# A mixture-of-experts stage padded to 256 slots per step: pairs of tiles share one first-layer matmul and one gelu

## What is computed

```python
gate_logits = x_flat @ gate_w.T
topk_vals, topk_idx = jax.lax.top_k(gate_logits, K)          # K = 2 of E = 8
topk_w = jax.nn.softmax(topk_vals, axis=-1)
...
for e in range(E):
    h = jax.nn.gelu(x_flat @ w1[e].T + b1[e], approximate=False)   # 128 -> 512
    y = h @ w2[e].T + b2[e]                                        # 512 -> 128
    out = out + comb[:, e:e + 1] * y
```

## Time and profile before

| | us |
|---|---|
| median of 3 timed executions | 423.61 |
| lowest and highest of these | 418.68, 425.56 |
| the profiled execution, its own time | 420.72 |
| its span (first to last instruction) | 418.8 |

### The profile page before, as it was taken

The page is one execution under the profiler, slowest core; times in us unless marked ns, Lnnn a source line. Parts: engine busy times, 40 slices in busy tenths (PEclk is TensorE's granted clock), DMA queues, the critical chain, the costliest instruction groups (busy, mean ns, idle before and its releaser), DMA issues.

```text
span 418.8 us, 5584 instructions
## 1 busy us (share of the span) xinstructions
PE 306.1 (73%) x1879; PEld 216.8 (52%) x1879; DVE 215.9 (52%) x457; ACT 159.8 (38%) x497; POOL 233.0 (56%) x214
## 2 busy tenths in 40 slices
PE   4988999799797309988759587586595883976244
PEld 1335443434236205467659487485584883975222
DVE  3733999999468897224324353143242441532066
ACT  4433020210125875035335363253453552634162
POOL 9100677979104340176767777767777777576300
PEclk9999897979998855599988999999999899899755
DMA  8900000000000150011111111111111111121296
GB/s 333 419 2 0 2 0 0 2 0 0 1 2 0 51 144 8 1 50 39 44 43 45 46 38 48 46 37 51 40 40 42 46 45 47 34 42 42 75 291 239
DMA packets 19484, 25.47 MB, mean 61 GB/s; under 512 B 2941, under 2 KB 15230, under 8 KB 19200
## 3 DMA queue, kind: packets, MB, share of 16 engines
q1 hardware_dynamic: 14336, 12.40, 9.4%
q0 software_dynamic: 4544, 8.86, 7.6%
q10 hardware_dynamic: 576, 3.86, 2.2%
HBM read 16.72 MB, written 8.85 MB: 61 GB/s over the span
## 4 chain that ended last, share of the span: by engine, by line
PE 45%; ACT 14%; DVE 13%; issue 9%; another core or an unknown queue 6%; DMA 6%; POOL 4%; SPq 2%; DVEq 0%; POOLq 0%
PE PS L1092 13%; PE PS L1099 12%; ACT MV L558 8%; DVE PR L689 4%; PE PS L1077 4%; PE PS L987 3%; ACT SCR L524 3%; PE PS L939 3%; PE PS L973 2%; DMA PR<-token_rows,dsti 2%; DMA X<-x 2%; POOL expert_rows L419 2%; SPq L345 2%; PE PS L1034 2%
## 5 line engine op out<-in xcount | busy, mean ns | idle before, releaser
L558 ACT ACTIVATE MV<-PS,SCR 128x128 f32<-128x128 f32 x284 | 81.3, 372 | 115.3 <-PE PS L1092 72.3
L1099 PE MATMUL PS<-SCR,MV 128*128 128x128 f32 x568 | 82.9, 291 | 48.3 <-ACT MV L558 33.6
L1099 PEld LDWEIGHTS PS<-SCR,MV 128*128 128x128 f32 x568 | 72.9, 201 | 57.0 <-ACT MV L558 40.3
L419 POOL DMA_INDIRECT expert_rows<-PR,dsti x71 | 80.6, 1135 | 37.7 <-issue 19.3
L413 POOL DMA_INDIRECT PR<-token_rows,dsti x71 | 76.5, 1077 | 40.9 <-issue 40.6
L1092 PE MATMUL PS<-MV,SCR 128*128 128x128 f32 x568 | 78.7, 284 | 0.0
L859 DVE TENSOR_TENSOR PR<-PS,SCR 128x128 f32<-128x128 f32 x71 | 20.6, 290 | 105.7 <-remote 61.6
L366 POOL TENSOR_TENSOR PR<-PR 128x1024 f32<-128x1024 f32 x21 | 49.5, 2362 | 42.9 <-DVE PR L689 41.2
L867 DVE COPY SCR<-WALL 128x1156 f32 x71 | 55.7, 788 | 34.1 <-DVE PR L859 23.2
L1092 PEld LDWEIGHTS PS<-MV,SCR 128*128 128x128 f32 x568 | 73.0, 201 | 0.0
L689 DVE TENSOR_TENSOR PR<-RX,PS 128x512 f32<-128x512 f32 x66 | 41.8, 677 | 5.1 <-PE PS L973 5.0
(11 more groups left out here) (167 smaller groups left out, 316.0 us busy)
## 6 DMA issues: line engine op xcount, KB each, us to landing
SCR<-expert_rows SPq DMA_DIRECT2D x16, 256.0 KB, 5.3
WALL<-experts SPq DMA_DIRECT2D x1, 2312.0 KB, 19.6
WALL<-experts ACTq DMA_DIRECT2D x1, 2312.0 KB, 19.8
token_rows<-SCR SPq DMA_DIRECT2D x4, 512.0 KB, 3.2
out<-PR SPq DMA_DIRECT2D x8, 256.0 KB, 2.4
PR<-token_rows,dsti POOLq DMA_INDIRECT x71
expert_rows<-PR,dsti POOLq DMA_INDIRECT x71
X<-x ACTq DMA_DIRECT2D x2, 512.0 KB, 6.2
```

The costliest lines, as they stand in the source:

```text
L419: nc.gpsimd.indirect_dma_start(yr, bass.IndirectOffsetOnAxis(ap=dsti[:, 2, q:q + 1].bitcast(U32), axis=0), YS[:, q % NR, :], None, bounds_ ...
L558: last = nc.scalar.activation(GF[:, q % 2, c * P:(c + 1) * P], PS[:, 2 + q % 2, c * P:(c + 1) * P], ACT.Gelu, bias=part(q, "b1")[:, c:c + 1])
L1099: last = nc.tensor.matmul(PS[:, 4 + q % 4, 0:C], GF[:, q % 2, c * P:(c + 1) * P], part(q, "w2")[:, c * C:(c + 1) * C], start=(c == 0), sto ...
```

## The change

The slots of an expert are now padded to a multiple of 256, so that two neighbouring tiles always belong to the same expert. They form a pair j, and all work but the transposes, the gathers and the scatters is done per pair. There are `NJ = (2 * T + E * 255) // 256 = 39` pairs, so 78 tiles for the 71 before.

- TensorE: `hidden(j)` is four matmuls that stream 256 columns each, into two PSUM banks; `output(j)` is eight matmuls (two tiles by four chunks) and newly waits for the add of pair j - 2, as results now share two banks and not four. `turn(j)` is two transposes.
- ScalarE: four gelus of 256 columns and one copy of 256 per pair.
- DVE: one weight copy per pair, and one add of 256 columns. The tile counts per expert are computed with 255 and a shift by 8, then doubled.
- GpSimd: 78 gathers and 78 scatters. Only the even ones wait, and they wait for their pair. `SLAG` is 8.
- The list of TensorE is `hidden(j)`, `turn(j + 2)`, `output(j - 1)` as before, with j a pair.

```diff
-NQ = (2 * T + E * (P - 1)) // P
+PAIR = 2 * P
+NJ = (2 * T + E * (PAIR - 1)) // PAIR
+NQ = 2 * NJ
...
-        XT = MV[:, 1, 0:4 * P].rearrange("p (s n) -> p s n", s=4)
-        GF = MV[:, 0, :].rearrange("p (s n) -> p s n", s=2)
+        XT = MV[:, 1, :].rearrange("p (s n) -> p s n", s=4)
+        GF = MV[:, 2:4, :]
...
-        SLAG = 7
+        SLAG = 8
...
+        def hidden_out(j, c):
+
+            at = (c % 2) * PAIR
+            return PS[:, 2 + 2 * (j % 2) + c // 2, at:at + PAIR]
...
             def gather(q):
-                if q >= NR:
-                    pool.wait_ge(xt_done, q - NR + 1)
+                if q >= NR and q % 2 == 0:
+                    pool.wait_ge(xt_done, (q - NR) // 2 + 1)
                     pool.sem_inc(pool_held, 1)
...
             def scatter(q):
-                pool.wait_ge(ys_done, q + 1)
-                pool.sem_inc(pool_held, 1)
+                if q % 2 == 0:
+                    pool.wait_ge(ys_done, q // 2 + 1)
+                    pool.sem_inc(pool_held, 1)
...
-            def gelu(q):
-                act.wait_ge(h_done, q + 1)
+            def gelu(j):
+                act.wait_ge(h_done, j + 1)
                 for c in range(HC):
-                    last = nc.scalar.activation(GF[:, q % 2, c * P:(c + 1) * P], PS[:, 2 + q % 2, c * P:(c + 1) * P],
-                                                ACT.Gelu, bias=part(q, "b1")[:, c:c + 1])
+                    last = nc.scalar.activation(GF[:, j % 2, c * PAIR:(c + 1) * PAIR], hidden_out(j, c),
+                                                ACT.Gelu, bias=part(j, "b1")[:, c:c + 1])
...
-            def finish(q):
-
-                dve.wait_ge(y_done, q + 1)
-                if q >= NR:
-                    dve.wait_ge(y_out[q % NR], 16 * (q // NR))
-                nc.vector.tensor_tensor(YS[:, q % NR, :], PS[:, 4 + q % 4, 0:C], part(q, "b2"), ALU.add).then_inc(ys_done, 1)
+            def finish(j):
+
+                dve.wait_ge(y_done, j + 1)
+                s = 2 * j % NR
+                if 2 * j >= NR:
+                    for r in (s, s + 1):
+                        dve.wait_ge(y_out[r], 16 * (2 * j // NR))
+                nc.vector.tensor_tensor(YS[:, s:s + 2, :], PS[:, 6 + j % 2, 0:2 * C].rearrange("p (i n) -> p i n", i=2),
+                                        part(j, "b2").unsqueeze(1).to_broadcast([P, 2, C]), ALU.add).then_inc(ys_done, 1)
...
-            def turn(q):
-
-                pe.wait_ge(g_in[q % NR], 16 * (q // NR + 1))
-                last = nc.tensor.transpose(PS[:, q % 2, 0:P], GX[:, q % NR, :], prm_("ident"))
+            def turn(j):
+
+                for i in range(2):
+                    q = 2 * j + i
+                    pe.wait_ge(g_in[q % NR], 16 * (q // NR + 1))
+                    last = nc.tensor.transpose(PS[:, j % 2, i * P:(i + 1) * P], GX[:, q % NR, :], prm_("ident"))
                 last.then_inc(xt_done, 1)
...
-            def output(q):
-                pe.wait_ge(gelu_done, q + 1)
-                for c in range(HC):
-                    last = nc.tensor.matmul(PS[:, 4 + q % 4, 0:C], GF[:, q % 2, c * P:(c + 1) * P],
-                                            part(q, "w2")[:, c * C:(c + 1) * C], start=(c == 0), stop=(c == HC - 1))
+            def output(j):
+                pe.wait_ge(gelu_done, j + 1)
+                if j >= 2:
+                    pe.wait_ge(ys_done, j - 1)
+                for i in range(2):
+                    for c in range(HC):
+                        a = c * PAIR + i * P
+                        last = nc.tensor.matmul(PS[:, 6 + j % 2, i * C:(i + 1) * C], GF[:, j % 2, a:a + P],
+                                                part(j, "w2")[:, c * C:(c + 1) * C], start=(c == 0), stop=(c == HC - 1))
                 last.then_inc(y_done, 1)
```

More of the change, by code:

```diff
@@ L319, in build, with part @@
         WLEAD = 2
-        SLAG = 7
-        def part(q, name):
+        SLAG = 8
+        def part(j, name):
             a, b = WX[name]
-            return WE[:, q % 4, a:b]
+            return WE[:, j % 4, a:b]
+        def hidden_out(j, c):
+            at = (c % 2) * PAIR
+            return PS[:, 2 + 2 * (j % 2) + c // 2, at:at + PAIR]
         block = ctx.enter_context(nc.Block())
@@ L548, in _, with turned @@
             nc.scalar.preload_act_table_set("gelu_and_others")
-            def turned(q):
-                act.wait_ge(xt_done, q + 1)
-                nc.scalar.activation(XT[:, q % 4, :], PS[:, q % 2, 0:P], ACT.Copy).then_inc(xtc_done, 1)
-            def gelu(q):
-                act.wait_ge(h_done, q + 1)
+            def turned(j):
+                act.wait_ge(xt_done, j + 1)
+                nc.scalar.activation(XT[:, j % 4, :], PS[:, j % 2, 0:PAIR], ACT.Copy).then_inc(xtc_done, 1)
+            def gelu(j):
+                act.wait_ge(h_done, j + 1)
                 for c in range(HC):
-                    last = nc.scalar.activation(GF[:, q % 2, c * P:(c + 1) * P], PS[:, 2 + q % 2, c * P:(c + 1) * P],
-                                                ACT.Gelu, bias=part(q, "b1")[:, c:c + 1])
+                    last = nc.scalar.activation(GF[:, j % 2, c * PAIR:(c + 1) * PAIR], hidden_out(j, c),
+                                                ACT.Gelu, bias=part(j, "b1")[:, c:c + 1])
                 last.then_inc(gelu_done, 1)
[L562 to L567, removed]
+            for j in range(TLEAD):
+                turned(j)
+            for j in range(NJ):
+                gelu(j)
+                if j + TLEAD < NJ:
+                    turned(j + TLEAD)
             act.wait_ge(gates_done, 2)
-            act.wait_ge(y_done, NQ)
+            act.wait_ge(y_done, NJ)
             for b in range(B):
@@ L805, in _ @@
             ntl, tend, off = (e8[:, k, :] for k in range(3))
-            chain(nc.vector.scalar_tensor_tensor(e8i[:, 0, :], ends, float(P - 1), begin, ALU.add, ALU.subtract))
-            chain(nc.vector.tensor_scalar(e8i[:, 1, :], e8i[:, 0, :], 7, None, ALU.arith_shift_right))
-            chain(nc.vector.tensor_copy(ntl, e8i[:, 1, :]))
+            chain(nc.vector.scalar_tensor_tensor(e8i[:, 0, :], ends, float(PAIR - 1), begin, ALU.add, ALU.subtract))
+            chain(nc.vector.tensor_scalar(e8i[:, 1, :], e8i[:, 0, :], 8, None, ALU.arith_shift_right))
+            chain(nc.vector.tensor_scalar(ntl, e8i[:, 1, :], 2.0, None, ALU.mult))
             chain(nc.vector.tensor_tensor_scan(tend, ntl, ntl, 0.0, ALU.add, ALU.max))
@@ L873, in _ @@
                 dve.wait_ge(rows_out[b], 16)
[L874 to L880, removed]
+            for j in range(WLEAD):
+                take_expert(j)
+            for j in range(NJ + OLAG):
+                if j + WLEAD < NJ:
+                    take_expert(j + WLEAD)
+                if j >= OLAG:
+                    finish(j - OLAG)
             dve.wait_ge(gates_done, 2)
@@ L1091, in hidden @@
                 for c in range(HC):
-                    last = nc.tensor.matmul(PS[:, 2 + q % 2, c * P:(c + 1) * P], part(q, "w1")[:, c * P:(c + 1) * P],
-                                            XT[:, q % 4, :], start=True, stop=True)
+                    last = nc.tensor.matmul(hidden_out(j, c), part(j, "w1")[:, c * P:(c + 1) * P],
+                                            XT[:, j % 4, :], start=True, stop=True)
                 last.then_inc(h_done, 1)
-            def output(q):
-                pe.wait_ge(gelu_done, q + 1)
-                for c in range(HC):
-                    last = nc.tensor.matmul(PS[:, 4 + q % 4, 0:C], GF[:, q % 2, c * P:(c + 1) * P],
-                                            part(q, "w2")[:, c * C:(c + 1) * C], start=(c == 0), stop=(c == HC - 1))
-                last.then_inc(y_done, 1)
@@ L1103, in _ @@
[L1103 to L1111, removed]
+            def output(j):
[7 more added lines that the diff above has]
+                                                part(j, "w2")[:, c * C:(c + 1) * C], start=(c == 0), stop=(c == HC - 1))
+                last.then_inc(y_done, 1)
@@ L1113, in _ @@
+            for j in range(TLEAD):
+                turn(j)
+            for j in range(NJ + OLAG):
+                if j < NJ:
+                    hidden(j)
+                if j + TLEAD < NJ:
+                    turn(j + TLEAD)
+                if j >= OLAG:
+                    output(j - OLAG)
             for b in range(B):
```

16 lines of the change are left out of this document (8 added, 8 removed).

## The result

The changed kernel takes 558.48 us (median of four runs, 556.57 to 559.20) against 423.25 us for the kernel before in the same comparison: a ratio of 1.324, with a 95% interval of 1.318 to 1.330. The forecast was 550 us. The profiled execution took 556.57 us for a span of 554.7.

The account below looks back on a forecast made before the run. A closed loop through GpSimd's and TensorE's lists was to bind the changed kernel: start 190.9, 35 rounds of 9.05 us (316.8), end 13.1, rest 27.05 and 1.9, giving 550 us against 420.72; range 506 to 591.

Parts of the forecast that it names:

- second layer 0 starts: Front of the stage: the first second layer waits for gather 7 and wider sorting, so starts at 190.9 us.
- 35 rounds: Expert stage, second layer 0 to 35: one closed loop per pair, 9.05 us each, 316.8 us.
- from there to the end of the span: After the last scatter starts: nothing changes, 27.05 us more to the span's end.
- The order decides: GpSimd and TensorE lists: second gather queues behind a scatter awaiting an add, closing a loop walked once per pair.
- The links of the round: Loop from second layer through add, scatter, gather, landing and transpose to the next second layer: 8.05 us.
- The clock: TensorE's second layer behind each pause meets the low 1.2 GHz level: 1.0 us more a round, making 9.05.
- The rival in which the clock holds: TensorE stays at full clock, the round stays 8.05 us: 515 us in all, chance 0.25.
- The end: Second layer 35, first layer 38, three second layers and last scatters: 13.1 us, last scatter starting at 520.8.
- Gelu and DMAs: Work per engine: four gelus 1.6 us a pair, 14 more GpSimd DMA instructions 18 us; none decides.
- The late results: Rival: each round's add comes 3 us late, the round is 12.05 us, 655 us in all; chance 0.06.
- the ring: Expert stage: the closed loop of second layer, add, scatter, gather, landing and transpose, walked once per pair, 8.05 us unthrottled.
- Issue-bound: Rival: the loop closes within GpSimd's 5.2 us a round, its 156 DMA instructions bind, 410 us; chance 0.04.

Follow-up runs that it names:

- four experiments: Changed kernel with both gathers first, scatters ten tiles behind, or second layer before transposes: 446.21, 451.11, 453.59 us; kernel before with scatters 3 tiles behind: 733.88 us.
- Filling the pause: Changed kernel with 24 unused matmuls of 256 fp16 columns before each pair's transposes: 523.58 us.
- the ring opened: Changed kernel with both gathers before both scatters, scatters ten tiles behind, or TensorE's second layer before the transposes: 446.21, 451.11 and 453.59 us.
- the exchange of two neighbours: Changed kernel with both gathers of a pair issued ahead of both scatters on GpSimd: 446.21 us.
- fp16 kernel: Kernel before with the operands of both expert layers in fp16, biases and sums in fp32: 416.33 us, ratio 0.986.
- filled pair kernel: Changed kernel with 24 unused matmuls of 256 fp16 columns in TensorE's pause before each pair's transposes: 523.58 us.
- Rings: Kernel before with 16 tiles in the buffers of gathered and result rows and scatters 12 tiles behind: 424.43 us, ratio 1.003.
- later second layers: Kernel before with 16-tile row buffers, scatters 12 tiles behind, and the second layer two tiles behind the first: 424.47 us.
- half the first layer: Kernel before with two of four first-layer chunks computed and the gelus reading each twice: 416.04 us.
- the fillers: Kernel before with five unused fp16 matmuls of 256 columns before each transpose, on another chip: 408.24 us against 405.00, ratio 1.008.

## Why the prediction was right, point by point

| term | forecast | measured |
|---|---|---|
| second layer 0 starts | 190.9 | 191.48 |
| 35 rounds | 316.8 (9.05 each) | 319.35 (9.12 each) |
| from second layer 35 to the last scatter | 13.1 | 527.02 - 510.83 = 16.2 |
| from there to the end of the span | 27.05 | 27.7 |
| the execution's own time above its span | 1.9 | 1.9 |
| sum | 550 | 556.57 |

*The order decides.* Right; four experiments bear it out, and 35 rounds were walked as counted. A slip changes nothing: the like loop before leads from tile q - 8 to q - 3, not from q - 7 to q - 2, which are five tiles too.

*The links of the round.* In the round shown: landing 2.53, landing to second layer 0.21, second layer to add 3.02, add 0.42, add to scatter 0.89, scatter to gather 1.56; together 8.63. The last four links, 0.21, 0.42, 0.89 and 1.56, came out as read from the kernel before. The landing was taken as 2.9; the chain of after puts 18.0% of 554.7 = 99.8 us on 36 landings, 2.77 each, though single ones reach 3.58. The Trainium skill's fixed part and bandwidth (DMA: Bandwidth & Descriptors, Anatomy of one DMA) give 2.15 as an estimate, below every landing in the chain above; the measurement decides.

*The clock.* It was taken as 1.0 us on top of 1.78 + 0.29. What is left of 9.12 after the other links is 9.12 - 2.77 - 0.21 - 0.42 - 0.89 - 1.56 = 3.27, so it was 1.2. Filling the pause removed 1.0. By the rule cited, every round pays; three rounds on the chain paid nothing (1.81 us for the layer). The two errors, -0.13 and +0.2, nearly cancel, as two guesses may; the sum owes that to luck. The rival in which the clock holds was wrong as a forecast, with 0.79 granted in the stage.

*The end.* This is the worst term, 3.1 us short. Behind second layer 35 the chain goes on with:

```profile
514.24 2.30 PE PS L1105 x8
516.54 1.78 PE PS L1116 x16
518.33 1.73 PE PS L1105 x8
520.06 3.73 PE PS L1116 x32
```

TensorE runs these back to back, as I had assumed, but there are two first layers in them and I had counted one. By the list, first layer 37 also comes after second layer 35; it is 2.3 us of the 3.1. Second layer 35 itself is 0.6 more (3.4 for 2.8). A first layer that is hidden in every round of the middle must be counted at the end.

*Gelu and DMAs.* The group of gelus has 475 ns for 256 columns, four in 1.57 us in the timeline (1.6 taken); the first layer 1.89 at full clock (1.78); the add 425 ns (0.42). None of it decided, as said.

*The late results* (0.06) didn't come: in the ring all 39 adds start 0.04 us after the second layer's records end. *Issue-bound* (0.04) would have needed a round under 5.2 us. Even with the ring opened the pair kernels stay at 446 to 454, not 410: 156 instructions at 2.60 a tile was too good a rate, since the kernel before itself ran at 3.03. The 27 us of the padding are seven tiles at 3.03 = 21, 3.3 for the front (first gather at 179.90 for 176.61), and some 3 that a single run doesn't resolve; I had said 18 + 2.

Together: of the 135 us, 27 are padding and 108 the ring (558.48 - 449.89), and of these 108 some 35 are the clock that the ring's pauses cost; the 27 and the 35 rest on one run each.

## What to carry to other kernels

In a program with hand-written lists, walk each cycle that goes through two in-order queues and count how many tiles lie between its start and its end: latency divided by that count is the rate, whatever the engines' busy shares say. Pairing work halves the number of steps but leaves the latency as it is, so the lags must be rewritten in the new unit; here the exchange of two neighbours gives back 112 us, and padding must then still be earned by something that the bound resource saves. If a TensorE group stands right behind a pause on the critical loop, count its clock, and if the pause can't be removed, small matmuls in it can be the cheaper evil.

## What was not expected of the hardware

**The chip matters by 4%, and TensorE's results can be late.** On two chips the kernel before took 421 to 423 us, on a third 405.0, with a spread of under 2% on each. On the slower ones, adds start up to 7.7 us, gelus of the fp16 kernel 9.8 us (above), after the last record of the matmuls they wait for, with the granted clock at 1.00 in the earlier trace rows; a profile on the third has no such delay in 71 tiles. The chip alone doesn't make it: in the closed rings, the kernel before with its lag of 3 and the filled pair kernel, every add follows 0.04 us behind the records, on the chip that gave 422.62. Rings, later second layers, half the first layer and fp16 gained nothing, nothing, 5 and 5 us of the possible 16 to 18. What the delay is stays open: there is no profile of the unchanged kernel on the third chip, and the fillers were in the only one that there is. That the chip, and not the fillers, took the delay away follows only from the time of 405.0 without them.

**A scatter beside a weight copy takes longer.** Held scatters take 1.25 us in the ring, where a DVE copy runs beside each (0.76 us from 301.66 for the scatter of 302.06), and 0.98 in the last ones, where no copy is left, though the one of 519.64 was held for an add too. The rule of the Trainium skill (SBUF — State Buffer, SBUF: two separate sides) that such a copy keeps GpSimd from writing descriptors fits both. It also fits the gathers, whose mean fell from 1077 to 980 ns, as the copies now lie beside the waits. No run moved the copies alone.

**fp16 for the experts** is the one version here that computes the whole stage and is below the kernel before beside it: 416.33 us for 420.97. The window of most of the stage, first of the kernel before, then of the fp16 kernel:

```profile
180.00:390.00 210.00, 154.35 (x1203) 143.39 (x1204) 72.02 (x137) 92.71 (x355) 152.28 (x138) 0.96 0.15 43
```

```profile
180.00:390.00 210.00, 91.98 (x643) 66.26 (x641) 77.46 (x208) 94.68 (x355) 152.95 (x141) 0.55 0.15 43
```

TensorE is busy for 92 us in place of 154, though at a granted clock of 0.55 for 0.96, and all of it bought 1.4% (0.6 to 2.2): its work alone was not the bound of the stage.
